# Bias attention: a block's maxima reach their row by two DRAM transfers instead of matmuls

## The reference, cut to what matters

```python
qkv = jnp.einsum('bhwc,cd->bhwd', x, w_qkv)
q, k, v = jnp.split(qkv, [qk_dims, 2 * qk_dims], axis=-1)
L = H * W
...
pos = relative_position_bias(pos_q, pos_emb_h, pos_emb_w).reshape(B, nh, L, L)
scores = jnp.einsum('bnqd,bnkd->bnqk', q, k) * scale + pos
attn = jax.nn.softmax(scores, axis=-1)
out = jnp.einsum('bnqk,bnkd->bnqd', attn, v)
```

## Time and profile before

| | |
|---|---|
| median of 3 runs | 9290.39 us (9289.0 to 9292.5) |
| the profiled execution | 9298.67 us, span 9296.3 us |
| busy share of the span | PE 90%, DVE 76%, ACT 62%, POOL 73% |
| busy, from 100 to 3200 us (bias attention) | PE 2887.00, DVE 2195.88, ACT 2410.05, POOL 2384.37 us |
| granted TensorE clock, from 100 to 3200 us | 0.97 |

### The profile page before, as it was taken

How to read it: one execution, slowest core, us unless ns; L and a number is a source line. 1 busy time by engine, 2 the same in 40 slices (tenths; PEclk the granted TensorE clock), 3 DMA queues, 4 the chain that set the end, 5 groups by cost and what they waited for, 6 DMA issues and landing times. The chain is left out here.

```text
span 9296.3 us, 140954 instructions
## 1 busy us (share of the span) xinstructions
PE 8381.5 (90%) x42548; PEld 6802.2 (73%) x42548; DVE 7037.8 (76%) x7884; ACT 5772.0 (62%) x14836; POOL 6757.5 (73%) x3644
## 2 busy tenths in 40 slices
PE   6999999999999676999999999968999989888798
PEld 4766767667677433888888888845887869888775
DVE  6776767767677565999999999965767746999734
ACT  4877878778787544777777777712665533445304
POOL 3876868768687644999999999910775734999704
PEclk8999999999999887999999999978999999888898
DMA  2111111111111245444444444452010110000000
GB/s 92 28 43 26 41 42 28 43 26 41 42 28 33 96 167 213 107 107 108 107 106 107 104 109 108 107 221 86 28 37 28 36 47 28 1 1 1 20 8 19
DMA packets 480131, 608.76 MB, mean 65 GB/s; under 512 B 273736, under 2 KB 294480, under 8 KB 469520
## 3 DMA queue, kind: packets, MB, share of 16 engines
q1 hardware_dynamic: 479504, 600.75, 22.6%
HBM read 349.14 MB, written 169.62 MB: 56 GB/s over the span
## 5 line engine op out<-in xcount | busy, mean ns | idle before, releaser
L817 POOL TENSOR_TENSOR l_probs_low<-l_probs,l_probs_high 128x512 fp32r<-128x512 f32 x1792 | 2384.4, 1359 | 790.2 <-ACT l_probs_high L787 774.5
L1542 POOL TENSOR_TENSOR m_c_h<-m_h,m_c 128x2048 f32<-128x2048 f32 x520 | 2341.5, 4562 | 47.2 <-DVE m_h L1529 47.1
L1529 DVE TENSOR_TENSOR_SCAN m_h<-m_decay,m_ps_x 128x1024 f32<-128x1024 f32 x1040 | 2270.8, 2262 | 94.6 <-issue 73.9
L1442 PE MATMUL m_ps_y<-m_c_h,m_ident 128*128 128x256 f32 x8320 | 1976.3, 381 | 2.1 <-POOL m_c_h L1542 2.1
L873 DVE TENSOR_REDUCE l_max_by_row<-l_ps_all 128x8 f32<-128x512 f32 x2048 | 1358.4, 685 | 525.6 <-PE l_ps_all L636 445.0
L1442 PEld LDWEIGHTS m_ps_y<-m_c_h,m_ident 128*128 128x128 f32 x8320 | 1510.0, 190 | 173.0 <-POOL m_c_h L1542 4.4
L785 ACT ACTIVATE l_probs<-l_ps_all 128x512 f32<-128x512 f32 x2048 | 1238.8, 605 | 454.8 <-PE l_ps_all L677 306.9
L787 ACT ACTIVATE l_probs_high<-l_ps_all 128x512 fp32r<-128x512 f32 x2048 | 1234.5, 603 | 0.0
L2093 POOL TENSOR_TENSOR l_probs_low<-l_probs,l_probs_high 128x512 fp32r<-128x512 f32 x512 | 659.7, 1292 | 666.0 <-ACT l_probs_high L2076 662.1
L2543 POOL TENSOR_TENSOR s_late<-s_late,s_products 128x1024 f32<-128x1024 f32 x352 | 858.2, 2482 | 309.5 <-ACT s_products L2525 309.5
L1466 ACT ACTIVATE m_b_diagonals<-m_steps,m_b_rows 128x32 fp32r<-128x32 f32 x4160 | 967.0, 306 | 3.1 <-DMA m_b_rows<-b_t 3.1
(11 more groups left out here) (376 smaller groups left out, 14204.3 us busy)
## 6 DMA issues: line engine op xcount, KB each, us to landing
m_delta_u<-du_t SPq DMA_DIRECT2D x1040, 128.0 KB, 3.8
m_c<-c_windows SPq DMA_DIRECT2D x130, 512.0 KB, 4.3
l_q_and_row_bias<-l_q_parts SPq DMA_DIRECT2D x64, 512.0 KB, 5.0
du_t<-m_delta_u_high SPq DMA_DIRECT2D x128, 256.0 KB, 3.0
du_t<-m_delta_u_low SPq DMA_DIRECT2D x128, 256.0 KB, 3.0
ys<-m_y SPq DMA_DIRECT2D x256, 126.0 KB, 5.0
m_direction<-ys SPq DMA_DIRECT2D x12, 2048.0 KB, 14.1
l_xn<-xn SPq DMA_DIRECT2D x8, 2048.0 KB, 7.9
```

The lines of the kernel that those rows point to most:

```text
L817: pool.tensor_tensor(pl[:, slot, :], pt[:, slot, :], f(ph[:, slot, :]), ALU.subtract).then_inc(low_pool, 1)
L1442: ins = pe.matmul(y_ps[:, group % 2, 0:DIRS * SPAN].rearrange("p (d t) -> p d t", d=DIRS), ident[:, :], ch[:, group % CH, :, n, :], start= ...
L1529: dve.tensor_tensor_scan(h[:, u % H, :], decay[:, pair % 2, ct, k % 2, :, :].rearrange("p n t -> p (n t)"), x_ps[:, u % X, :], 0.0, ALU.mu ...
L1542: pool.tensor_tensor(ch[:, group % CH, 2 * pair % DIRS:2 * pair % DIRS + 2, :, :].rearrange("p d n t -> p d (n t)"), h[:, 2 * pair % H:2 * ...
```

## The change

TensorE turns the maxima only for a head's first block. For the other seven, SP stores `mx` to a row `maxima` in DRAM and loads that row again, repeated, into 64 partitions of a new buffer `max_wide` (`spread_maxima`), and the shift subtracts this. DVE's due time for the shift goes from 19.3 to 25.3, and DVE waits for its own reduction at the end of `take_maxima`.

```diff
--- before.py
+++ after.py
@@ -390,7 +390,7 @@
                 normalise(t)
 
 
-def bias_attention(nc, stage, xn, att, w_heads, emb_h, emb_w, cells_in, ident_in, sums, inverses):
+def bias_attention(nc, stage, xn, att, w_heads, emb_h, emb_w, cells_in, ident_in, sums, inverses, maxima):
 
 
 
@@ -464,6 +464,8 @@
         const, parts_ok, tables_ok = m.sem("const"), m.sem("parts_ok"), m.sem("tables_ok")
         image_in, w_in, qm_in, last_in = m.sem("image_in"), m.sem("w_in"), m.sem("qm_in"), m.sem("last_in")
         filled, copied, split = m.sem("filled"), m.sem("copied"), m.sem("split")
+        max_wide = m.sb("max_wide", [SIDE, TW])
+        max_out, max_in = m.sem("max_out"), m.sem("max_in")
         max_filled, max_taken, max_ok = m.sem("max_filled"), m.sem("max_taken"), m.sem("max_ok")
         bias_turned, turned, own, shifted = m.sem("bias_turned"), m.sem("turned"), m.sem("own"), m.sem("shifted")
         ql_in = [m.sem("ql_in0"), m.sem("ql_in1")]
@@ -532,6 +534,14 @@
                 for g in range(GROUPS):
                     for first, part in ((D, rh), (D + NEAR, rl)):
                         sp.dma_start(f(ql[first:first + NEAR, slot, g, :]), f(part[g * NEAR:(g + 1) * NEAR, :])).then_inc(ql_in[slot], 16)
+
+            def spread_maxima(it, j):
+                n = it * (NTB - 1) + (j - 1)
+                sp.wait_ge(max_ok, it * NTB + j + 1)
+                sp.wait_ge(shifted, it * NTB + j + 1)
+                sp.dma_start(maxima.rearrange("a (c p) -> p (a c)", p=P), mx[:, :], allow_slow_non_contiguous=True).then_inc(max_out, 16)
+                sp.wait_ge(max_out, n * 16 + 16)
+                sp.dma_start(max_wide[:, :], maxima.to_broadcast((SIDE, TW))).then_inc(max_in, 16)
 
             def send_sums(row):
                 sp.wait_ge(summed, row + 1)
@@ -573,6 +583,7 @@
                             sp.dma_start(xs[:, :], xn[:, b * L:(b + 1) * L]).then_inc(image_in, 16)
                             sp.dma_start(w[:, :], w_heads[h * P:(h + 1) * P, :]).then_inc(w_in, 16)
                     if j + 1 < NTB:
+                        spread_maxima(it, j + 1)
                         copy_rows(it, j + 1)
             send_sums(ITS * NTB - 1)
             spread_inverses(ITS * NTB - 1)
@@ -710,8 +721,6 @@
                     if j + 1 < NTB:
                         if i == 4:
                             turn_bias(row + 1, j + 1)
-                        if i == READY:
-                            turn(row + 1)
                     if i + 2 < KT:
                         score(it, j, i + 2)
                     elif j + 1 < NTB:
@@ -878,11 +887,17 @@
                 turned_bias = ps[:, TURNED, 0:QT * SIDE].rearrange("p (t x) -> p t x", x=SIDE)
                 chain.link(dve.tensor_tensor(mx64[:, :, :], mx64[:, :, :], turned_bias, ALU.add))
                 dve.tensor_reduce(mx[:, :], mx64[:, :, :], AX.X, ALU.max).then_inc(max_ok, 1)
+                dve.wait_ge(max_ok, row + 1)
 
             def shift(row):
-                j = row % NTB
-                dve.wait_ge(turned, row + 1)
-                chain.link(dve.tensor_tensor(r1[:, :], r32[:, j * TW:(j + 1) * TW], ps[0:SIDE, TURNED, :], ALU.subtract))
+                it, j = row // NTB, row % NTB
+                if j:
+                    dve.wait_ge(max_in, (it * (NTB - 1) + j) * 16)
+                    largest = max_wide[:, :]
+                else:
+                    dve.wait_ge(turned, it + 1)
+                    largest = ps[0:SIDE, TURNED, :]
+                chain.link(dve.tensor_tensor(r1[:, :], r32[:, j * TW:(j + 1) * TW], largest, ALU.subtract))
                 if row:
                     dve.wait_ge(ql_in[(row - 1) % 2], ((row - 1) // 2 + 1) * QL_LOADS + 1)
                 chain.link(dve.tensor_copy(rh[:, :], r1[:, :]))
@@ -937,7 +952,7 @@
                     for i in range(KT):
                         work += [(i + 0.8 + 0.05 * k, reduce_unit, it * NTB + block_of, u) for k, (block_of, u) in enumerate(units(j, i))]
                     if j + 1 < NTB:
-                        work += [(READY + 0.1, take_maxima, row + 1), (READY + 0.3, shift, row + 1)]
+                        work += [(READY + 0.1, take_maxima, row + 1), (READY + 6.3, shift, row + 1)]
                     elif it + 1 < ITS:
                         work += head(it + 1, lambda tile: tile)
                     in_order(work)
@@ -3054,7 +3069,7 @@
     xn0, att = act_map("xn0"), act_map("att")
     group_norm(nc, "gn0", a["x"], xn0, a["group_mean"], 1e-5)
     bias_attention(nc, "l0", xn0, att, a["w_heads"], a["emb_h"], a["emb_w"], a["cells"], a["ident"],
-                   dram("sums", 1, TW), dram("inverses", 1, TW))
+                   dram("sums", 1, TW), dram("inverses", 1, TW), dram("maxima", 1, TW))
 
     x1, xn1, x2 = act_map("x1"), act_map("xn1"), act_map("x2")
     group_norm(nc, "gn1", a["x"], xn1, a["group_mean"], 1e-5, addend=att, x_sum=x1)
```

## The result

The changed kernel takes **9794.15 us** (median of 4 runs, 9782.04 to 9801.39) beside 9291.44 for the kernel before: a ratio of 1.0533, 95% interval 1.0516 to 1.055. It is slower, as forecast, but by 503 us where 220 were forecast, and above the range. Its profiled execution has a span of 9799.3 us at a mean clock of 0.915.

A forecast was written before the change was run, and what follows sets the result against it. TensorE was taken as the bound. Ordinary blocks 131 us, block 1 55 and block 6 35, clock losses included, make 221 more than the median 9290.39: 9511 us, range 9400 to 9600.

The forecast's parts named there:

- the sum: Forecast total: ordinary blocks 131, block 1 55, block 6 35, together 221 us more; ordinary wait 0.8 on DVE, 2.4 at score.
- The shift's place, M + 5.95: DVE's shift starts 5.95 us after M, the end of DVE's reduction to the maxima, behind tile 24's unit.
- The copies, 6.9 us: Eight row-bias copies on SP behind the shift: 6.9 us from the shift's end until the rows are in.
- The turn's 1.94: TensorE's turn of the maxima, four matmuls and their wait, costs 1.94 us a block.
- The image ahead of block 1's store: Next head's 2 MB image, 7.9 us to land, delays block 1's store: wait 7.9, net 6.0, in 7 blocks.
- Block 6: No later units behind its maxima; TensorE waits 4.5 us at the score, net 2.5, in 8 blocks.
- the store at 1.8 us: Store of 512 single elements to DRAM, interpolated between `inverses` at 1.4 us and `b_t` at 4.5.
- rival B: Maxima late, at most M + 8.9; DVE waits for them in every block: 9595 us, or 9676 with both ends; chance 0.10.
- The shift at 2.45 us: DVE's shift between maxima and row copies takes 2.45 us, with a cast of 1.17 in it, shortest 0.42.
- The clock at 1.9 a block: TensorE's clock falls to half after the wait in all 56 blocks, losing 1.9 us each.
- Rival A: The clock holds over the short waits, so 41 × 1.9 = 78 us go: 9433 us; chance 0.22.
- The gain of 109 us: Removing TensorE's turn from 56 of 64 blocks saves 56 × 1.94 = 109 us, if nothing new is late.

The follow-up runs named there:

- e2: The kernel before with only DVE's due time for the shift moved, 25.3 instead of 19.3, the turn kept: 9518.44 us, ratio 1.023.
- e1: The changed kernel with the store in 128 runs of 16 bytes, DVE restoring the order by a strided read: 9493.18 us, ratio 1.0199.
- e10b: e1 with GpSimd held until DVE's shift is done and the next head's image issued behind block 1's copies: 9323.62 us, ratio 1.0027.
- the probe: The kernel before with small transfers timed singly ahead of the layer: 512 single elements 10.3 us, runs of 16 bytes 1.4; total not compared.
- e8: The kernel before with the turn one tile later in TensorE's program, nothing else: 9298.18 us, ratio 1.0002.
- e9b: e10b with the maxima formed two tiles earlier and GpSimd held ahead of tile 22 instead of 24: 9296.42 us, ratio 1.0000.

## Why the prediction missed

**What held.** The direction, and its reason: the moved shift, and the eight copies behind it. e2, which moves only these, loses 0.023 × 9307 = 214 us, and the score waits for the rows in nearly every block; e1, with the store made cheap, loses 186 where the sum had 221. The shift's place, M + 5.95: measured M + 5.84 in e1. The copies, 6.9 us from the shift's end: 685.03 to 691.44 in e1, 6.4, in mid-block. The load, 2.9 to 4.3: 4.3, the upper end, in the changed kernel, and 3.6 in e1. The turn's 1.94, as a local cost. The image ahead of block 1's store: the store took 12.8 us there (661.06 to 673.86), and in e10b it is 39 us that it costs once the rest is repaired, against 55 in the sum, which read the image's issue as 1.5 us before M (595.64 − 594.67 is 0.97). Block 6 as the score's own wait, in kind: 12.3 us instead of 4.5. The clock's fall in all blocks.

**The step that failed: the store at 1.8 us, ends 1.4 and 4.5.** It took 9.2. I interpolated between `inverses` and `b_t` by the number of pieces. Both rows write runs of 16 bytes or more, and the probe shows the price to depend on something neither has, single elements beside each other. The step took them as the ends of the unknown; a kind of access that no row shows has no end there. By the ratios of the two kernels, each to its own kernel before, the cheap store is worth (1.0533 − 1.0199) × 9300, some 310 us, and that though e1's shift is 2.3 us longer than the changed kernel's.

**By it, rival B came true beyond its own bounds.** The maxima are there at M + 13.5 instead of at M + 5.2, B's farthest being M + 8.9. B's mechanism, DVE waits for `l_max_wide` in every block, is what the trace shows.

**Where the wait falls.** The sum put 0.8 us of it on DVE and 2.4 at the score. It is 7.9 ahead of a unit, and at most 1.3 at the score in ordinary blocks, because the rows land while TensorE stands and then works at half clock. The forecast's own sentence, that the two banks fill while DVE reduces nothing, was right and sized too small.

**The shift at 2.45 us in mid-block was wrong for e1's reason, not for the changed kernel's.** There it took 1.85 since GpSimd stood too. With the store as forecast it is 4.2 in the usual block and 5.25 in the one shown. The earlier trace rows had the sign of it: the cast on line 888 with a shortest of 0.42 and a median of 1.17. I took the median and did not ask what makes it vary between them.

**The clock at 1.9 a block** measured 2.7 in the changed kernel; some 0.8 × 56 = 45 us of the miss. This is read from the trace, and no run isolated it. Rival A, that the clock holds over short waits, can't be told from the forecast in the changed kernel, whose stops are three times as long as forecast. e1 has them at 2.2 us. After the one that ends at 728.79 the clock falls to 0.50, after the one that ends at 772.71 it doesn't:

```profile
731.00:733.00 2.00, 2.00 (x6) 1.51 (x6) 0.56 (x2) 1.08 (x2) 1.09 (x2) 0.50 0.15 33
772.00:777.00 5.00, 3.98 (x16) 2.93 (x16) 4.06 (x7) 3.06 (x6) 4.58 (x4) 1.00 0.16 39
```

So at the size of wait that was forecast, neither the fall everywhere nor A holds in full.

**The gain of 109 us did not come.** "TensorE is the bound, so all of it counts" fails in e8, for the 43 us that TensorE waits at the turn. For the other 66, the turn's own products, e9b is the only evidence, and it also holds GpSimd back and forms the maxima earlier; no run takes away the products alone. TensorE is busy 97% of the steady stretch, but DVE and its two banks are so close behind that a stall removed comes back at the next unit. The slowdown was forecast as 109 gained and 330 lost; in the runs nothing was gained.

**The rule cited.** The prediction set beside its rivals the rule of the Trainium skill, DMA: Bandwidth & Descriptors, to issue early and wait late; it stands there in "Rules for kernel authors". By it the change gains. In the runs it holds for the load itself, which in e1's ordinary blocks DVE doesn't wait for, and what it leaves out is the work that depends on the transfer: the shift and the copies moved back with the wait, and e1 loses 186 us though the turn is gone.

## What to carry to other kernels

Before a small transfer to DRAM is put on a path that something waits for, lay out the DRAM side so that each partition writes its elements as one run, and let the reader's access pattern restore the order: here that was 9.2 us against 1.45 for the same 2 KB. A stall on the busiest engine is worth what it lasts only if the engine that empties its banks next has slack at that very place: move the waiting instruction by a tile first, which is one line, and see whether the time moves. Work on DVE that lies in one piece longer than its banks can buffer stops TensorE wherever it stands, and its length is to be read from a stretch in which GpSimd does what it will do there. Here holding GpSimd back for the three instructions was worth 0.013 of the time.

## What the hardware showed that I had not expected

- Storing 128 single 4-byte elements into 512 contiguous bytes took 7.9 to 9.6 us in three rounds, 512 of them 9.8 to 11.6, 512 at a spacing of 64 bytes 2.0 to 2.8, 128 runs of 16 bytes 1.4 but for the first, 2.9; reading the 512 back took 2.1 to 2.3.
- The same DVE cast of 64x512 took 0.42 us with GpSimd idle and 1.39 to 1.43 with it busy; the same subtraction 0.68 and 1.63 to 1.65. With one operand in PSUM the subtraction stayed at 0.67. Where DVE's instruction started just ahead of GpSimd's, it was GpSimd's that grew, from 1.29 to 2.21.
- Around the stop of 8.1 us the granted clock fell from 1.00 to 0.50 3.4 us after the last matmul, and was back 5.8 us after the work, where the stop that the prediction used had 3.9.
